# A fused cross-attention and mixture-of-experts kernel: schedule written earlier, silu ahead of copies, gate products inside a tile, two copies of experts' last rows behind each load

## The reference, cut to what matters

```python
q = relu(layernorm(x) @ Wq + bq);  k = relu(ctx @ Wk + bk);  v = relu(ctx @ Wv + bv)
x = x + relu((relu(q @ k.T) / sqrt(512) + mask) @ v)
z = layernorm(x)
logits = z @ gate_w                      # 8 experts
topv, topi = top_k(logits, 2);  w = softmax(topv)
Y[e] = (silu(z @ Wu[e]) * (z @ Wv[e])) @ Wo[e]      # 512 -> 128 -> 512
x = x + sum over the two chosen experts of w * Y[e]
```

## Time and profile before

| | |
|---|---|
| median of three executions | 422.38 us |
| the profiled execution: its time | 421.33 us |
| its span | 419.5 us |
| PE busy | 398.1 us, 95% |
| DVE busy | 331.8 us, 79% |
| ACT busy | 277.3 us, 66% |
| POOL busy | 213.1 us, 51% |
| mean granted clock of PE | 0.99 |
| DMA traffic | 87.13 MB, mean 208 GB/s |
| idle time of PE until a DMA's end, at tile 25's turning | 1.1 us |

### The profile page before, as it was taken

One profiled execution on the slowest core, in us unless ns is written; L12 is line 12 of the kernel. 1 busy time (PEld: TensorE's weight loads), 2 busy tenths in 40 slices (PEclk: granted clock), 3 DMA queues, 4 the chain that ended last, 5 costly groups with the idle time before them and its releaser, 6 DMA issues.

```text
span 419.5 us, 10234 instructions
## 1 busy us (share of the span) xinstructions
PE 398.1 (95%) x3031; PEld 356.1 (85%) x3031; DVE 331.8 (79%) x1108; ACT 277.3 (66%) x596; POOL 213.1 (51%) x224
## 2 busy tenths in 40 slices
PE   8999999999999999998989899989999999999990
PEld 5689999999999999997778789889999999999970
DVE  2668899999999999999868888868887666666650
ACT  1677888888889988886677566656676444444420
POOL 2011125656665656564556743323333464888872
PEclk9999999999999999999999999999999999999995
DMA  8821336776766666545795468869965699999793
GB/s 288 276 65 62 102 102 205 249 251 232 246 206 229 213 230 247 179 155 171 250 309 212 181 189 258 275 218 312 293 224 178 200 227 270 311 276 135 97 130 52
DMA packets 49509, 87.13 MB, mean 208 GB/s; under 512 B 7600, under 2 KB 18352, under 8 KB 49328
## 3 DMA queue, kind: packets, MB, share of 16 engines
q1 hardware_dynamic: 35600, 52.37, 39.7%
q0 software_dynamic: 13856, 34.10, 29.2%
HBM read 43.98 MB, written 48.29 MB: 220 GB/s over the span
## 4 chain that ended last, share of the span: by engine, by line
PE 70%; DVE 6%; SPq 6%; issue 5%; ACT 4%; DMA 4%; POOL 2%; POOLq 1%; ACTq 0%
PE psQ L1453 12%; PE psQ L1454 12%; PE psQ L1455 12%; PE psT L1449 11%; PE psO L1453 2%; PE psO L1454 2%; PE psO L1455 2%; PE psZ L1453 2%; SPq L541 2%; PE psZ L1455 2%; PE psZ L1454 2%; PE psS L1453 2%; PE psQ L1449 2%; PE psG L1549 2%; PE psS L1455 2%
## 5 line engine op out<-in xcount | busy, mean ns | idle before, releaser
L900 DVE TENSOR_TENSOR qT<-psT,qT 128x512 fp32r<-128x512 f32 x103 | 69.5, 688 | 29.2 <-ACT qT L708 29.1
L612 POOL DMA_INDIRECT z_dram<-zb x64 | 72.4, 1132 | 31.5 <-DVE zb L1188 16.2
L1453 PE MATMUL psQ<-wuv,qT 128*128 x284 | 86.3, 304 | 0.0
L1454 PE MATMUL psQ<-wuv,qT 128*128 x284 | 80.5, 283 | 0.0
L1455 PE MATMUL psQ<-wuv,qT 128*128 x284 | 80.2, 282 | 0.0
L1453 PE MATMUL psQ<-qT,wq 128*128 128x256 f32 x256 | 75.2, 294 | 1.5 <-DVE qT L900 1.5
L1455 PE MATMUL psQ<-qT,wq 128*128 128x256 f32 x256 | 72.4, 283 | 0.0
L1454 PE MATMUL psQ<-qT,wq 128*128 128x256 f32 x256 | 72.3, 283 | 0.0
L708 ACT ACTIVATE qT<-psT 128x512 fp32r<-128x512 f32 x103 | 59.5, 595 | 15.0 <-PE psT L1449 15.0
L1453 PEld LDWEIGHTS psQ<-wuv,qT 128*128 128x128 f32 x284 | 53.7, 189 | 4.9
L776 ACT ACTIVATE gate_work<-psQ 128x128 f32<-128x128 f32 x71 | 19.6, 277 | 52.8 <-PE psQ L1455 52.8
(11 more groups left out here) (299 smaller groups left out, 1061.3 us busy)
## 6 DMA issues: line engine op xcount, KB each, us to landing
wq_flat<-z_dram SPq DMA_DIRECT2D x28, 264.0 KB, 4.0
xin<-in_x_dram SPq DMA_DIRECT2D x11, 512.0 KB, 3.9
z_dram<-spare SPq DMA_DIRECT2D x17, 264.0 KB, 3.9
qpT_flat<-z_dram SPq DMA_DIRECT2D x11, 264.0 KB, 3.6
zT_ctxT<-in_x_dram SPq DMA_DIRECT2D x5, 512.0 KB, 3.5
kpT_flat<-z_dram SPq DMA_DIRECT2D x9, 264.0 KB, 3.7
vp_flat<-z_dram SPq DMA_DIRECT2D x9, 264.0 KB, 4.5
xn<-z_dram SPq DMA_DIRECT2D x8, 264.0 KB, 3.7
```

What stands on the lines that cost most here:

```text
L612: pool.indirect_dma_start(out=z_dram, out_offset=bass.IndirectOffsetOnAxis(ap=z_of(b)[:, t, ROW_COL + k:ROW_COL + k + 1].bitcast(U32), axi ...
L900: nc.vector.tensor_tensor(o, a, b, ALU.subtract).then_inc(s, 1)
L1453: pe.matmul(o, w[LO], a[HI], start=first, stop=False)
L1454: pe.matmul(o, w[HI], a[LO], start=False, stop=False)
```

## The change

On SP, two copies instead of one stand behind each load, so all eight lie between the loads of tiles 17 and 21. On DVE, `know_pads` moves from tile 7 to tile 11; `keep_sched(0)` moves ahead of the routing of block 12 (`choose.all`) and of `logits_low` in block 15; in block 14 the planning of part 0 moves ahead of `keep_stats`. On PE, the turning of part 0's schedule waits for `s_relu` (ACT's relu of block 14's scores) in place of `lg_ready` (DVE's masked sum, which comes later), and the gate products of block 14 move from a place ahead of tile 2 to one inside it, behind `down(1)`. On ACT, the silu of tiles 1 and 2 moves ahead of the copies `turned_z` of block 14.

```diff
@@ SP, tiles @@
-                if EARLY <= t < EARLY + E:
+                if EARLY <= t < EARLY + E // 2:
                     if t == EARLY:
                         sp.wait_ge(pads_known, 2)
                         sp.wait_ge(head_stored, 16 * E)
-                    copy_tail(t - EARLY)
+                    for e in range(2):
+                        copy_tail(2 * (t - EARLY) + e)
@@ ACT, after the blocks @@
             turned_s(0)
+            gate(1)
             turned_z(last + (-1), 0, psS)
-            gate(1)
             turned_g(3)
             turned_s(1)
+            gate(2)
             turned_z(last + (-1), 1, psS)
             again(0)
             norm2(last, 0)
             gate_logits(last + (-1))
-            gate(2)
             turned_g(4)
@@ DVE, body(b) @@
                 if prv.real:
                     masked(prv)
+                if b.n == EARLY_NB + 3:
+                    keep_sched(0)
                 if third.real:
                     choose.all()
                 if prv.real:
                     logits_low(prv)
                 if b.n == EARLY_NB + 3:
                     plan_used(0)
-                    keep_sched(0)
...
-                if prv.real:
-                    keep_stats(prv)
                 if ends_early:
                     plan_ends(0)
                     plan_rows(0)
+                if prv.real:
+                    keep_stats(prv)
@@ DVE, tiles @@
                     dve.wait_ge(place, PLACE_STEPS * NB)
-                    know_pads()
                     plan_lengths(1)
...
                 if t == 11:
+                    know_pads()
                     lists_sizes()
@@ PE @@
                 if g == 0:
-                    pe.wait_ge(lg_ready, NB - 1)
+                    pe.wait_ge(s_relu, NB - 1)
...
                     down(t - 1, expert_of(t - 1))
                     del expert[t - 1]
+                if t == 2:
+                    gates(Step(NB - 2))
...
             turn_z(last + (-1), 1, psS)
-            gates(last + (-1))
             tile_body(2)
```

## The result

The changed kernel takes 425.30 us, the median of five executions (424.70 to 427.24), against 422.00 us for the kernel before beside it (five, 421.12 to 422.92): a ratio of 1.0082 [1.0052, 1.0112]. It is slower by 3.3 us. The profiled execution is the longest of the five, 427.24 us with a span of 425.5 us, 6.0 us over the span of before.

What follows compares the result with a forecast made beforehand. It took TensorE, busy 95% of the span, as the bound; 0 - 0.17 - 0.14 + 7.0 - 1.09 = +5.6 us on 421.33 gave 426.9, and 428.0 us as median, range 424.8 to 430.8.

Steps and rivals of the forecast that it cites:

- part 0's schedule, tile 1: PE's 1.59 us gap moves ahead of block 14's attention; tile 1's 0.47 us load wait stays: 0 us.
- tile 2: PE's gaps at tile 2: 0.17 of 0.93 us goes, 0.76 stays as one wait for `gated(2)`: -0.17 us.
- tile 8: DVE's stretch before PE's 1.76 us gap loses two `know_pads` places 0.07 us apart: -0.14 us.
- tiles 9 to 15: `know_pads` at tile 11 falls ahead of `gated(12)`, where PE has no gap: 0 us.
- waits for loads: PE waits at tiles 19 to 21 because tile 21's load is 4.6 to 7.3 us late: +7.0 us taken.
- clock: No clock loss in the sum; a rival had PE at 1.2 GHz after the last stall, 2.7 us more.
- tile 25: The eighth copy lands sooner, so PE's 1.09 us wait for tile 25's load goes: -1.09 us.
- Schedule, silu, gate products: Moves up to tile 2: schedule gap moved, not removed, 0 us; gaps at tile 2 shrink, -0.17 us.
- SP's queue: Copies delay SP's loads: first copy at 249.19, tile 21's load at 267.63 at the fastest, 270.2 with slower reads.
- it lands 4.3 us later: Landing of tile 21's load after issue: 4.3 us, or 5.1, giving 271.9 to 274.5 against PE's turning at 267.28.
- the rival with 0.06: PE's clock falls to 1.2 GHz after the last stall; a tile costs 2.7 us more: 430.7 us; chance 0.06.
- From execution to median: From 426.9 us for a profiled execution to a 428.0 us median, adding before's 1.05 us of median over profile.

Runs made afterwards that it cites:

- two_only: The kernel before with two copies instead of one behind each load, nothing else changed: 425.77 us, ratio 1.0078.
- one_late: The changed kernel with one copy behind each load again, the copies' numbers still made at tile 11: 423.81 us, ratio 1.0043.
- rest_only: The changed kernel with one copy behind each load and `know_pads` at tile 7 again, all else kept: 421.85 us, ratio 0.9988.
- numbers_at_7: The changed kernel with `know_pads` back at tile 7, still two copies behind each load: 425.96 us, ratio 1.0092.
- the first four experiments: two_only, rest_only, numbers_at_7 and one_late, run on one chip beside 18 executions of the kernel before, which took 422.33 us.
- read_early_one_at_8: The changed kernel with SP reading the sixteen numbers before tile 17's load, `know_pads` at tile 8, one copy per load: 432.53 us, ratio 0.9983.

## Why the prediction was right or wrong

Direction and cause were right, the time was within the range, and the size of the median was not: +3.3 us instead of +5.6. The steps in turn, for the profiled execution:

| term | predicted | measured |
|---|---|---|
| part 0's schedule, tile 1 | 0 | -0.20 at down(0) |
| tile 2 | -0.17 | -0.28 |
| tile 8 | -0.14 | -0.54 |
| tiles 9 to 15 | 0 | -0.28 |
| waits for loads | +7.0 | +5.49 |
| clock | 0 (a rival) | +3.1 |
| tile 25 | -1.09 | -1.27 |
| sum | +5.6 | +6.0 |

**Schedule, silu, gate products: right.** The gap moved in front of `lgT`, 1.59 us before and 1.65 after; the attention starts at 194.50, where about 194.5 was forecast. Tile 2 keeps one gap before its gated values, 0.97 us, where 0.76 was forecast and 0.93 us stood in two gaps before. So the gaps there didn't shrink. Even so 0.28 to 0.33 us were gained from `down(0)` to `down(7)` in all four profiles with these moves (0.13 us in `two_only`, without them); from what, no run tells. The gap of 0.47 us at tile 1 was to stay and is absent; the profiles of the first chip have 0.76, 0, 0.29 and 0.24 us there (in the table's order), so it varies by more than the change could move it.

**`know_pads`: mis-sized.** The step was "two places 0.07 us apart", -0.14 us. It was worth 0.54 us in the changed kernel and in `one_late`. Timeline of DVE at tile 8, before:

```profile
236.07 0.36 DVE L938 TENSOR_SCALAR len_i<-cnt_i 128x8 int32<-128x8 int32 x1
236.46 0.17 DVE L943 TENSOR_TENSOR length<-len_i,used 128x8 f32<-128x8 int32 x1
236.89 0.29 DVE L1200 TENSOR_TENSOR gate_work<-gate_work,psQ 128x128 f32<-128x128 f32 x1 [0.26 <-DVE length L943]
```

and after:

```profile
235.46 0.17 DVE L939 TENSOR_SCALAR len_i<-cnt_i 128x8 int32<-128x8 int32 x1
235.66 0.17 DVE L944 TENSOR_TENSOR length<-len_i,used 128x8 f32<-128x8 int32 x1
235.87 0.29 DVE L1201 TENSOR_TENSOR gate_work<-gate_work,psQ 128x128 f32<-128x128 f32 x1
```

Beside the two places, 0.2 us went from the one instruction and 0.26 us of idle time vanished. It is no accident of one execution: all four profiles near 422 us with the numbers at tile 7 have 0.36 us and an idle time of 0.26 or 0.27 us there, both with the numbers at tile 11 have 0.17 us and none. Why, no run tells. More weighty is what came with it: at 1.22 us the clock held in both profiles, at 1.76 to 1.78 us it fell in three of four, for 1.45 us.

**SP's queue: right in its times.** Put into the clock of before (1.30 us added), the first copy goes out at 249.44 (249.19 forecast) and the load of tile 21 at 270.01 (270.2 forecast); the first copy waited 1.2 us for its numbers (1.40). **The term that was mis-sized is the landing:** "it lands 4.3 us later". Behind two copies the four loads took 3.2 to 3.6 us. So tile 21's rows are there at 273.2 in the clock of before, 5.9 us after 267.28, not 7.0; and 5.49 us of it were waited. The rule of the Trainium skill ("DMA: Bandwidth & Descriptors", section "Queues, rings and completion order") would have made them later than those with one copy ahead. No row shows it: the loads of tiles 18 to 21 took 3.2 to 3.6 us in the changed kernel and 3.3 to 3.7 in `two_only`, and with one copy ahead 3.0 to 4.3 in `rest_only` and 2.9 to 4.5 in `one_late`. The figure chosen was simply one of many: in the profile of before the loads of tiles 17 to 25 took from 2.9 to 5.1 us. What makes them differ is not known.

**The clock: the rival with 0.06 happened.** Half clock took 3.1 us in the changed kernel, against the rival's 2.7. From the table in the same way (from `down(15)` to `down(21)`, less the waits) it took 1.7 us in `two_only` and 1.6 in `numbers_at_7`. The argument for 0.06 was one row: a gap of 1.76 us with the clock at 1.00. Three other executions with that gap at tile 8 say the contrary. One row of one execution showed that the clock can hold, not that it does. The Trainium skill ("TensorE: Matmul & The Clock Gate", section "HAM oscillation — how this bites in real kernels") warned that waits for DMAs tile by tile bring the half clock, and the trace agrees in part: 0.50 behind the second long wait, but 1.00 behind the first.

**Tile 25: right,** -1.27 for -1.09 us.

**From execution to median: wrong.** The profiled sum was nearly met, 427.24 us against the 426.9 forecast for an execution like that of before, but by 1.5 us too much of waiting and 3.1 us of clock that canceled. To it I added the 1.05 us by which the median of before stands above its profile, as though that carried over. It is the other way round: the profile after stands 1.9 us above its median, that of before 0.7 to 1.0 us below. One may think of the clock at tile 8: other executions of before may pay 1.45 us that the profiled one did not. They have no profile, but their mean granted clock is on record. It is 0.990 in the profiled execution of before and 0.986 in that of `rest_only`, which paid. Of the 18 executions of before beside the first four experiments, 8 have 0.986 or 0.987; they took 422.7 us on average, the other ten 422.2 us. So perhaps less than half have paid, and only some 0.5 us goes with it. That explains little of the difference; the rest stays open. The changed kernel's profile is one of two long executions (427.17 and 427.24 us, the other three 424.70 to 425.30), so the 6.0 us taken apart above are not the 3.3 us of the medians. Besides, waits and lateness cancel: an execution that is late at tile 15 waits less for its loads.

**What stays open.** On the first chip the kernels that read early were not run, so whether `read_early_one_at_8` beats before there, where tile 25's wait is 1.1 us and not 0.7, is not known. A version with `masked` moved ahead as well was not tried.

## What to carry to other kernels

A transfer whose address comes from memory costs the queue that issues it mostly its reads: here 1.7 to 2.5 us for a copy with two numbers, 0.4 to 1.0 us if the numbers are in registers. Count the queue's time between two loads against the consumer's time for a tile before putting more on it: 5.1 to 6.1 us against 2.7 us could not hide here. And price a stall of TensorE from several executions, since the same gap may or may not bring the half clock with it, and the half clock cost here 0.6 to 1.1 times the gap on top of it.

## What the runs showed of the hardware that was not expected

- In the profiles of before, of the changed kernel and of the first four experiments the granted clock fell to 0.50 in or behind gaps of PE of 2.84 us (0.50 till 278, 3.1 us lost), 2.74 and 2.63 us, of 1.77 us (tile 20 of `numbers_at_7`), and of 1.76 to 1.78 us at tile 8 in three of four profiles (1.45 us lost). It held behind 2.46 us in the changed kernel, and behind 1.65, 1.22 and 1.07 us. So the length of a gap alone doesn't tell.
- The same program takes 422 us on one chip and 433 to 434 us on three others, with five waits of ACT for something remote between 200 and 262 us, 14.35 us together on the chain that ends last.
- Loads of 264 KB landed no later behind two copies (3.2 to 3.7 us in the changed kernel and `two_only`) than behind one (2.9 to 5.1 us in before, `rest_only` and `one_late`).
- SP with its numbers in registers issues a copy 0.4 to 1.0 us after a load, where with two numbers to read it is 1.7 to 2.4 us.
- Two instructions of DVE on 1x8 values, 0.07 us apart, ahead of a chain made it end 0.54 us later: the next instruction took 0.36 us in place of 0.17 us, and 0.26 us of idle time came with it (four profiles with them, two without).
